# Attention's loop entered after half of the first batch's scores, with the rest and the second batch's projections inside its first steps

## What is computed

```python
x = x + tanh(g_xattn[0]) * _L0_xattn_ref(_layernorm(x), ctx_2048, mask_SxS2_bc0, mask_BxS2_bk0, Wq, bq, Wk, bk, Wv, bv, Wo, bo)

def _L0_xattn_ref(X, enc, causal_mask, padding_mask, Wq, bq, Wk, bk, Wv, bv, Wo, bo):
    q, k, v = X @ Wq.T + bq, enc @ Wk.T + bk, enc @ Wv.T + bv     # 32 query heads, 8 groups of keys and values, 16 wide
    scores = einsum('bgrqd,bgkd->bgrqk', q, k) / sqrt(16), masked twice with -inf
    w = softmax(scores)
    return einsum('bgrqk,bgkd->bgrqd', w, v).reshape(b, LQ, 512) @ Wo.T + bo
```

## Time and profile before

| | us |
|---|---|
| median of 3 runs | 1663.49 (1662.81 to 1663.49) |
| the profiled execution | 1660.81 |
| its span | 1659.1 |
| TensorE busy in the span | 1576.7 (95%) |
| the attention, from the start to the last `times_v` | about 493 |
| the prologue, to the first `turned_scores` | 77.7 |

### The profile page before, as it was taken

One profiled execution on the slowest core, in us unless ns is written; L12 is line 12 of the kernel. 1 busy time (PEld: TensorE's weight loads), 2 busy tenths in 40 slices (PEclk: granted clock), 3 DMA queues, 4 the chain that ended last, 5 costly groups with the idle time before them and its releaser, 6 DMA issues. The chain is left out here.

```text
span 1659.1 us, 29208 instructions
## 1 busy us (share of the span) xinstructions
PE 1576.7 (95%) x10826; PEld 828.4 (50%) x10826; DVE 944.3 (57%) x1947; ACT 710.2 (43%) x1311; POOL 831.6 (50%) x893
## 2 busy tenths in 40 slices
PE   5889999999779999999999989999999999999998
PEld 3456665666434444446565644444444444444443
DVE  5756766778847888735656442468454333322246
ACT  3288888888886666523323221211111111233321
POOL 3488887877884555533534244434342542022244
PEclk9899999999899999999999999999999999999999
DMA  7754645333254665433553427546453745388855
GB/s 189 169 119 100 119 94 110 89 80 75 73 130 95 127 121 102 96 83 77 109 124 80 96 65 159 119 97 158 90 108 92 153 111 115 77 190 195 188 154 189
DMA packets 453955, 195.67 MB, mean 118 GB/s; under 512 B 395500, under 2 KB 418286, under 8 KB 453816
## 3 DMA queue, kind: packets, MB, share of 16 engines
q1 hardware_dynamic: 440216, 171.26, 47.6%
q0 software_dynamic: 5680, 18.62, 4.4%
q10 hardware_dynamic: 7920, 3.93, 1.0%
HBM read 77.17 MB, written 22.81 MB: 60 GB/s over the span
## 5 line engine op out<-in xcount | busy, mean ns | idle before, releaser
L1143 POOL TENSOR_TENSOR a_pl<-a_prob,a_ph 128x512 f16<-128x512 f32 x256 | 296.0, 1170 | 74.6 <-ACT a_prob L1032 74.2
L1232 DVE TENSOR_REDUCE a_mx<-bank 128x2 f32<-128x512 f32 x256 | 173.2, 686 | 87.2 <-PE bank L730 85.7
L140 PE MATMUL bank<-XTh,d_whs 128*128 128x512 f16 x512 | 194.9, 381 | 3.9 <-PEq L89 2.4
L141 PE MATMUL bank<-XTl,d_whs 128*128 128x512 f16 x512 | 194.7, 380 | 0.0
L142 PE MATMUL bank<-XTh,d_wls 128*128 128x512 f16 x512 | 194.6, 380 | 0.0
L1031 ACT ACTIVATE a_ph<-bank 128x512 f16<-128x512 f32 x256 | 153.8, 601 | 59.2 <-PE bank L750 36.2
L2420 POOL CAST d_cut<-d_raw 128x512 f16<-128x512 f32 x90 | 57.1, 635 | 227.4 <-DMA d_raw<-in_L_ffn_sw 145.6
L1032 ACT ACTIVATE a_prob<-bank 128x512 f32<-128x512 f32 x256 | 154.0, 602 | 0.0
L2340 DVE TENSOR_TENSOR d_hid<-d_hid,bank 128x512 f32<-128x512 f32 x64 | 43.9, 686 | 169.2 <-PE bank L142 165.3
L2331 ACT ACTIVATE d_hid<-bank 128x512 f32<-128x512 f32 x64 | 38.2, 597 | 204.9 <-PE bank L142 204.9
L2335 ACT ACTIVATE d_hh<-d_hid 128x512 f16<-128x512 f32 x64 | 40.3, 630 | 194.2 <-DVE d_hid L2340 194.2
(11 more groups left out here) (350 smaller groups left out, 3978.1 us busy)
## 6 DMA issues: line engine op xcount, KB each, us to landing
d_raw<-in_L_ffn_w SPq DMA_DIRECT2D x48, 256.0 KB, 3.0
d_raw<-in_L_ffn_sw SPq DMA_DIRECT2D x42, 256.0 KB, 3.0
made<-e_y SPq DMA_DIRECT2D x39, 256.0 KB
a_stage<-in_L_ffn_w_fc SPq DMA_DIRECT2D x32, 256.0 KB, 2.9
a_stage<-in_L_ffn_w_proj SPq DMA_DIRECT2D x32, 256.0 KB, 3.0
a_fbuf<-in_ctx SPq DMA_DIRECT2D x16, 256.0 KB, 3.2
rows<-f_cut SPq DMA_DIRECT2D x16, 256.0 KB, 2.5
out_x<-X SPq DMA_DIRECT2D x16, 256.0 KB, 2.4
```

The source lines that it names most:

```text
L140: nc.tensor.matmul(out_ap, lhi, rhi, start=first, stop=False)
L141: nc.tensor.matmul(out_ap, lhi, rlo, start=False, stop=False)
L1143: nc.gpsimd.tensor_tensor(pl[:, n % NP, :], prob[:, n % 2, :], ph[:, n % NP, :], ALU.subtract).then_inc(ev["L"], 1)
L1232: nc.vector.tensor_reduce(mx[:, h, tt, half, 2 * (g % 4):2 * (g % 4) + 2], bank[BS + m % 2][:, :].rearrange("p (r k) -> p r k", r=2), AX_X ...
```

## The change

The loop of batch 0 is entered after 16 of the 32 score tiles and after the first of the two projections of queries, and of keys and values, of batch 1. The rest goes into batch 0's loop: two tiles of batch 0's second half in each of steps 0 to 7, `q_of(1, 1)` in steps 0 to 3, `kv_of(1, 1)` in steps 4 and 5, the four `turn_k` of batch 1 in steps 8 to 11, the second `turn_maxima` in step 9. Batch 1's 32 score tiles, one in each of steps 0 to 31 before, stand in steps 10 to 31, so one or two in a step.

SyncE's stream follows: `place_x(2)`, `load_ctx(3)`, `place_q(1, 0)` and `place_maxima(0, 1)`, in the prologue before, stand in steps 6 to 10 of batch 0. `place_ctx` is split into the transposes and the stores (`store_ctx`). `x`'s load of 2560 KB stands behind `place_ctx(2)`, `place_maxima(0, 0)` and `store_ctx(2)`, no longer ahead of all three; the three first pieces stay behind it. GpSimd's four instructions for `x` of batch 2 move from the prologue to steps 1, 2, 4 and 5. Batch 3's context and `x`, and the output weights, come some steps later in batch 0's loop; `place_x(3)` stands behind `place_maxima(1, 0)` and no longer ahead of it.

```diff
-    WO_AT = [12, 14, 16, 18]
+    WO_AT = [14, 15, 22, 23]
+    HALF = NS // 2
+    SECOND, Q1_AT, KV1_AT, K1_AT = 8, 0, 4, (8, 9, 10, 11)
+    NEXT_AT = 10
+    MAX1_AT = 9
+    X2_AT = (1, 2, 4, 5)
+    def first_scores(n):
+        if n < SECOND:
+            return [(0, m) for m in range(HALF + 2 * n, HALF + 2 * n + 2)]
+        steps = NS - NEXT_AT
+        upto = [max(0, -(-(i - NEXT_AT) * NS // steps)) for i in (n, n + 1)]
+        return [(1, m) for m in range(*upto)]
...
         load_ctx(2)
+        place_ctx(2)
+        place_maxima(0, 0)
+        store_ctx(2)
         sp.dma_start(X[:, 6:16, :], x_tiles[:, 6:16, :]).then_inc(x_in[3], 16)
-        place_ctx(2)
         sp.wait_ge(g_tr, 2)
         for l in range(NST):
             load_piece(l)
-        place_q(1, 0)
-        place_maxima(0, 0)
-        place_x(2)
-        load_ctx(3)
-        place_maxima(0, 1)
...
+                if b == 0 and n == X2_AT[3] + 1:
+                    place_x(2)
+                    load_ctx(3)
+                if b == 0 and n == KV1_AT + 3:
+                    place_q(1, 0)
+                if b == 0 and n == MAX1_AT + 1:
+                    place_maxima(0, 1)
+                    place_q(1, 1)
-                if f < B and n == 10:
+                if f < B and n == (10 if b else 17):
                     place_ctx(f)
+                    store_ctx(f)
...
-                if f < B and n == 22:
+                if f < B and n == (22 if b else 28):
                     place_x(f)
...
-        for m in range(NS):
-            if m in (6, 12):
-                q_of(1, m // 12)
-            if m in (9, 15):
-                kv_of(1, m // 15)
-            if m == 18:
-                wait("lq1", 1)
-                turn_maxima(0, 0)
-            if m in (22, 26):
-                turn_k(1, (m - 22) // 4, 0)
+        for m in range(HALF):
             scores(0, 0, m)
+        turn_maxima(0, 0)
         wait("nc", 0, 1)
-        turn_maxima(0, 1)
+        q_of(1, 0)
+        kv_of(1, 0)
...
-                if more:
+                if b == 0:
+                    for c, m in first_scores(n):
+                        scores(c, c, m)
+                    if Q1_AT <= n < Q1_AT + KC:
+                        q_of(1, 1, [n - Q1_AT])
+                    if n in (KV1_AT, KV1_AT + 1):
+                        kv_of(1, 1, [2 * (n - KV1_AT), 2 * (n - KV1_AT) + 1])
+                    if n in K1_AT:
+                        turn_k(1, K1_AT.index(n) % 2, K1_AT.index(n) // 2)
+                    if n == MAX1_AT:
+                        wait("lq1", 1)
+                        turn_maxima(0, 1)
+                elif more:
                     scores(b + 1, 1 - par, n)
```

More of the change, by code:

```diff
@@ L590, in on_sp @@
         place_ctx(0)
+        store_ctx(0)
         load_ctx(1)
@@ L1152, in body @@
                 if b + 3 < B:
-                    if n == 5:
+                    if n == (5 if b else 13):
                         deviation(b + 3)
-                    if n in FRONT:
-                        part_of, t = FRONT[n]
+                    if b == 0 and n in X2_AT:
+                        t, low = X2_AT.index(n) // 2, X2_AT.index(n) % 2
+                        (x_low if low else x_high)(2, t)
+                    late = n if b else n - 7
+                    if late in FRONT:
+                        part_of, t = FRONT[late]
                         part_of(b + 3, t)
@@ L1337, in on_dve @@
                 take(0, tt, h, "k")
-        for m in range(NS):
-            if m == 18:
-                moments(2)
-            if m == 22:
+        moments(2)
+        for m in range(HALF):
+            if m == 4:
                 mean(2)
-            if m in (8, 14):
-                low_q(1, m // 14)
-            if m in (11, 17):
-                low_kv(1, m // 17)
-            if m in (23, 27):
-                take(1, (m - 23) // 4, 0, "k")
             maxima(0, m)
+        low_q(1, 0)
+        low_kv(1, 0)
         def body(b, par, more, more2):
@@ L1377, in body @@
                     front_clip(g)
-                if more:
+                if b == 0:
+                    for c, m in first_scores(n):
+                        maxima(c, m)
+                    if n == Q1_AT + KC:
+                        low_q(1, 1)
+                    if n == KV1_AT + 2:
+                        low_kv(1, 1)
+                    if n in K1_AT:
+                        take(1, K1_AT.index(n) % 2, K1_AT.index(n) // 2, "k")
+                elif more:
                     maxima(b + 1, n)
```

32 lines of the change are left out of this document (18 added, 14 removed).

## The result

| | before | changed |
|---|---|---|
| median of 12 runs each, us | 1663.49 (1656.62 to 1666.80) | 1670.12 (1665.66 to 1676.47) |
| the profiled execution, us | 1660.81 | 1671.25 |
| its span, us | 1659.1 | 1669.5 |

The ratio changed to before is 1.0044, with a 95% interval of 1.0030 to 1.0057: the change makes the kernel 0.44% slower, by 6.6 us in the medians (5.0 to 9.5 us by the interval). 1669.2 us had been predicted.

What follows compares the result with a forecast made beforehand. It took TensorE, busy 45.8 to 49.8 us of some 52 us per pass, to bound the loop. B1 4.7 us later plus 1.0 us in batch 1 gave +5.7 us on 1663.49, so 1669.2 us; range 1659.5 to 1675 us.

Steps and rivals of the forecast that it cites:

- both waits it named: Batch 0's loop: ScalarE waits some 8 us for the first weight piece, TensorE 6 to 8 us for batch 1's queries.
- Steps 1 to 3: Prologue: last maximum ends at 57.0 us, first turned tile at 64.4 us; prologue 13.3 us shorter (up to 17.3).
- Step 4: x's big load issued at 61.4 us, landing 13.1 us later; first weight piece there at 75.3 us (73.9 to 76.6).
- Steps 5 and 6: Batch 0's loop: ScalarE stands until 75.3 us for the first weight piece; `absolute(1)` ends 7.7 us later, at 83.7 us.
- Step 7: SyncE's issues behind `absolute(1)` take 13.3 us; batch 1's queries land at 97.0 us, TensorE waiting from about 90 us.
- Step 8: Batch 0's loop, from batch 1's first score tile in loop step 10 to B1: 37.6 us (36 to 40).
- B1: First turned score tile of batch 1, at 129.92 us before; predicted at 134.6 us, 4.7 us later.
- Step 9: Batch 1: GpSimd waits 1.2 us for batch 4's later context load; 1.0 us taken as the cost.
- rival D: TensorE falls to the lower clock in both waits of batch 0 and stays there: +12, 1675 us; chance 0.08.
- Rival B: Weight pieces do not wait behind the big load: B1 at 126.8 us, 1661.4 us, faster or the same; chance 0.15.
- Rival C: Both waits in batch 0 are covered: B1 at 121.1 us, -7.8 us in all, 1655.7 us; chance 0.12.

Runs made afterwards that it cites:

- run 1: Changed kernel with the first three pieces of weights issued ahead of x's big load; ratio to the kernel before 1.0001.
- run 4: Changed kernel with x's big load back in its old place, behind the load of batch 2's context; ratio to the kernel before 1.0005.
- run 6: run 5 with half of SyncE's issues ahead of batch 1's queries moved to steps 2 and 3 of batch 0; ratio to the kernel before 0.9947.
- run 10: Changed kernel with only the edit of run 6 to SyncE's issues, big load still ahead of the pieces; ratio to the kernel before 0.9988.
- run 5: Changed kernel with the big load in its old place and batch 4's context load in step 28 of batch 0; ratio to the kernel before 1.0007.
- run 7: run 6 with two of four pairs of output weight transposes ahead of the loop instead of in steps 14 and 15; ratio to the kernel before 0.9953.
- run 2: Changed kernel with batch 1's query transposes issued ahead of x's transposes and context load of batch 3; ratio to the kernel before 1.0014.
- run 3: Changed kernel with batch 4's context load in step 28 of batch 0, ahead of batch 3's x transposes; ratio to the kernel before 1.0024.
- run 8: Changed kernel with the big load issued by ScalarE on its own queue, behind the copy of the maxima; one time, 1666.68 us.

## Why the prediction was right, and where its terms were off

The sum, 1669.2 us, stands 0.9 us from the median and inside the interval, and the mechanism is the one it rested on: both waits it named are there, and removing the first (runs 1 and 4) or the second (runs 6 and 10) gave at least its time back. Several terms were off, and in part against each other.

- **Steps 1 to 3** were too slow by 3.2 us. After the moments VectorE's maxima ran at 0.65 us each; 0.80 us, from the stretch at the lower clock, never came. The last ended at 54.6 us, the faster bound being 54.9. The entry was at 61.25 us, 16.5 us earlier than before instead of 13.3.
- **Step 4**, the big load, was issued at 61.2 us (61.4 predicted) and took 10.3 us, not 13.1. The bound that I had worked out from its bytes and the queue's rate, 73.9 us for piece 0, was nearer to the 72.2 us than the value chosen (its own terms, 9.9 us of transfer and 2.8 of landing behind 61.4, add up to 74.1). That the 13.1 us of the row held other transfers too is only argued. The Trainium skill, DMA: Bandwidth & Descriptors (Anatomy of one DMA), would have 8.0 us by its fit, an estimate, from DMAs that GpSimd issues; the 10.3 us measured lie between it and the row of before. In the ten runs the load took 10.4 to 12.8 us: 11.9 to 12.8 in its old place (runs 4 to 7), 10.4 to 11.7 behind the stores with the pieces behind it (2, 3 and 10). Where I said that what is issued behind the load waits until the load is through, the effect is right (run 1) and the reason too narrow (run 8): it does so on another queue as well.
- **Steps 5 and 6** held: ScalarE stood 7.3 us (8 predicted), TensorE 5.0 us, and `absolute(0)` to `absolute(1)` took 7.6 us (7.7).
- **Step 7** held: from the end of `absolute(1)` to TensorE's first score tile 13.8 us (13.3), a wait of 7.3 us (6 to 8). Only its moment, 94.4 us instead of 97.0, carried over what steps 1 to 4 had wrong.
- **Step 8** is the first mis-sized term: 40.3 us, not 37.6 (I had gone up to 40). The windows from TensorE's first score tile in step 10 (step 10's turned tile in the kernel before) to B1, of the kernel before, of the changed kernel and of run 7, split the error:

```profile
92.36:129.92 37.56, 32.84 (x420) 19.92 (x421) 20.71 (x40) 31.91 (x71) 30.30 (x29) 1.00 0.60 121
```

```profile
94.38:134.66 40.28, 37.60 (x450) 24.69 (x451) 30.18 (x57) 29.28 (x64) 28.63 (x28) 0.94 0.55 116
```

```profile
82.40:121.50 39.10, 35.81 (x452) 23.45 (x451) 29.89 (x57) 30.21 (x66) 30.62 (x31) 1.00 0.55 120
```

  At the full clock, in run 7, TensorE's busy time is 3.0 us above that of before, close to the 3.2 us counted for the ten tiles; but only 1.4 us of its idle time took this up, where I let it take nearly all. The other 1.2 us go with the clock, at 0.59 us a matmul behind the wait at 94.38 us (a granted share of 0.50 up to 98.90 us), which I had looked for only in step 6; run 6 against run 7 prices such a stretch of 3.3 us at 1.6 us. The length was 40.3 to 40.6 us in runs 1, 3 to 6, 8 and 10 as well, whenever the queries came. And run 7 took four transposes out of SyncE's stream from step 14 on and B1 moved by 0.2 us, so SyncE, to whom I had given an equal part in setting B1, does not set it. These 2.7 us cancelled the early start: B1 is at 134.66 us, predicted 134.6. That this one number is right to 0.1 us is luck.
- **Step 9** is the other mis-sized term: 5.0 us in the profiled execution where I took 1.0. The wait was the one named, 2.2 us (1.2 predicted), and runs 3 and 5 to 7, which have no wait for this load, still take 1.0 to 1.3 us more than before, which I had not foreseen (in each of them GpSimd stands 0.8 to 1.0 us at the same place for a transpose of `x` of batch 3, and nothing there before); what I did not count at all is the clock that falls behind such a wait, 3 us. That is rival D's mechanism in another place than I looked for it.
- **Rival B** was close once its condition was made true: with the pieces first, `absolute(1)` ended 12.0 us after the entry (11.5 said), the queries were there at 89.9 us (89.2) and the kernel was level with the one before (1.0001, where B had 2.1 us less). B1 was at 130.4 us and not at 126.8, nearly all of it the mis-sized term of step 8. Its condition, that the pieces do not wait behind the load, was false.
- **Rival C** needed piece 0 in time and a chain 7 us shorter. Run 6 makes both true by moving issues, and gave 0.53% over before, where C said 7.8 us or 0.47%.

The sum of B1 and batch 1 in the traces is +9.7 us against +5.7 predicted, while the medians say 6.6. The 3 us between them are of the size by which the two profiled executions lie apart from their medians (3.8 us). That the sum came within 0.9 us of the median is thus luck in part as well: the entry was 3.2 us better than reckoned, steps 8 and 9 were 2.7 and 4.0 us worse, and the medians lie closer together than the traces. Whether every execution of the changed kernel shows the fall of the clock in batch 1 was not measured; their mean clocks go from 0.977 to 0.982, the fastest execution having the highest.

## What to carry to other kernels

Work taken out of a prologue brings forward every need behind it, so go through what the first steps of the loop wait for and ask of each whether its transfer was issued that much earlier too. Small loads that are needed at once go ahead of a large one that is not: that took the wait away (run 1). A second queue for the large one did not (run 8), the small ones still needed 9.3 us. And where an in-order issuing engine has to wait for a signal, put what is already ready ahead of the wait, down to half a batch of transposes: here that was worth 0.6%, more than the 0.44% by which the change had moved the time.

## What the runs showed that I had not expected

- A load of 2.62 MB holds small transfers on other queues as well: 256 KB issued 4 us later by another engine, behind 0.5 MB of stores, needed 9.3 us instead of about 3, and for the first 5 us of the load the other queue was not served at all.
- It also holds the issuing engine: with the load in flight four transposes took 10.1 us to be issued instead of 5.1 us. In run 4, whose context transposes stand behind the load, single ones took up to 2.5 us (up to 2.9 us in the kernel before, where they stand so too) instead of 1.3 us in the changed kernel:

```profile
47.04 1.22 SPq L538 DMA_TRANSPOSE a_cTh<-a_fcut  x1
48.30 2.24 SPq L539 DMA_TRANSPOSE a_cTl<-a_fcut  x1
50.59 2.46 SPq L538 DMA_TRANSPOSE a_cTh<-a_fcut  x1
```

- Waits of 1.7 to 2.2 us on another engine, with equal work around them, cost this kernel 1 us in two executions and 4 us in three, by whether TensorE's granted clock stayed at 1.00 or fell to 0.65 to 0.67 over the next 9 us.
